# The last output projection in two parts, and the last batch's receptance mixing on VectorE

## The reference

```python
x = x + attn(layernorm(x))        # 16 heads, keys of 16, values of 64, softmax over the queries' axis
x = x + xattn(ctx, ctx, layernorm(x))   # 16 heads of 16, features exp(z) and exp(-z), then fc_w and fc_b
x = x + ffn(layernorm(x))

def ffn(x):                       # x_prev is x shifted by one position, zero first
    xr = mu_r * x + (1.0 - mu_r) * x_prev
    xk = mu_k * x + (1.0 - mu_k) * x_prev
    r = sigmoid(xr @ W_r.T)
    k_act = square(relu(xk @ W_k.T))
    return r * (k_act @ W_v.T)

def attn(x):
    sim = einsum('bnkh,bmhk->bnhm', q, k)
    p = softmax(sim / 4, axis=1)
    o = einsum('bnhm,bmhv->bnhv', p, v)
    return einsum('bnhv,dhv->bnd', o, output_proj)
```

## Time and profile before

| | us |
|---|---|
| median of 3 runs | 449.89 (449.42 to 451.17) |
| the profiled execution's time | 449.9 |
| its span, first to last instruction | 448.1 |
| busy TensorE, VectorE | 426.5, 367.7 |
| busy ScalarE, GpSimd | 300.9, 161.2 |

### The profile page before, as it was taken

One profiled execution on the slowest core, in us unless ns is written; L12 is line 12 of the kernel. 1 busy time (PEld: TensorE's weight loads), 2 busy tenths in 40 slices (PEclk: granted clock), 3 DMA queues, 4 the chain that ended last, 5 costly groups with the idle time before them and its releaser, 6 DMA issues.

```text
span 448.1 us, 8243 instructions
## 1 busy us (share of the span) xinstructions
PE 426.5 (95%) x2738; PEld 274.4 (61%) x2738; DVE 367.7 (82%) x668; ACT 300.9 (67%) x760; POOL 161.2 (36%) x206
## 2 busy tenths in 40 slices
PE   6999999999989999999999999999999999879896
PEld 4745454466545865566655785576555674467775
DVE  4688877798998887888999978798999888669762
ACT  3687988676796666666778566666787757529521
POOL 2163203117232513427052622427331533534442
PEclk9999999999999999999999999999999999999999
DMA  7668302435210015145103002642003100000001
GB/s 241 234 236 269 142 1 96 143 107 197 75 47 1 1 55 179 64 150 187 45 6 119 0 2 103 197 153 91 0 1 111 57 1 1 23 2 1 1 25 47
DMA packets 22561, 38.23 MB, mean 85 GB/s; under 512 B 2808, under 2 KB 7160, under 8 KB 22392
## 3 DMA queue, kind: packets, MB, share of 16 engines
q1 hardware_dynamic: 22520, 37.71, 24.6%
HBM read 23.02 MB, written 14.68 MB: 84 GB/s over the span
## 4 chain that ended last, share of the span: by engine, by line
PE 75%; DVE 9%; ACT 8%; issue 4%; DMA 1%; POOL 1%; SPq 0%; POOLq 0%; ACTq 0%; DVEq 0%
PE av_bank L909 22%; PE m_bank L841 9%; PE s_pair L895 8%; PE m_bank L845 6%; DVE nmax L1355 4%; ACT e_sb L1148 3%; PE m_bank L1045 3%; PE m_bank L961 2%; PE m_bank L1057 2%; PE m_bank L982 2%; PE m_bank L1117 2%; PE m_bank L1106 2%; PE m_bank L926 2%; PE m_bank L1073 2%; PE m_bank L945 1%
## 5 line engine op out<-in xcount | busy, mean ns | idle before, releaser
L1148 ACT ACTIVATE e_sb<-s_pair,nmax 128x512 f32<-128x512 f32 x256 | 174.1, 692 | 62.0 <-DVE nmax L1355 61.8
L1355 DVE TENSOR_REDUCE nmax<-s_pair 128x2 f32<-128x1024 f32 x128 | 152.4, 1213 | 21.5 <-PE s_pair L895 20.6
L909 PE MATMUL av_bank<-e_sb,v_sb 128*64 128x512 f32 x512 | 120.1, 602 | 1.0 <-POOL v_sb L1627 0.8
L1627 POOL TENSOR_TENSOR v_sb<-v_sb,rsum 128x256 f32<-128x256 f32 x64 | 39.7, 622 | 156.6 <-DVE rsum L1363 156.6
L909 PEld LDWEIGHTS av_bank<-e_sb,v_sb 128*64 128x64 f32 x512 | 32.6, 136 | 62.8 <-issue 53.2
L895 PE MATMUL s_pair<-q_st,k_st 64*128 64x512 f32 x256 | 49.9, 456 | 4.8 <-ACT e_sb L1148 4.8
L1148 ACT ACTIVATION_READ_ACCUMULATOR e_sb<-s_pair,nmax 128x1 f32 x256 | 53.6, 209 | 0.0
L895 PEld LDWEIGHTS s_pair<-q_st,k_st 64*128 64x128 f32 x256 | 21.3, 184 | 39.1 <-ACT e_sb L1148 25.2
L841 PE MATMUL m_bank<-wo_hi,ot_hi 128*128 128x256 f32 x128 | 36.4, 290 | 0.0
L845 PE MATMUL m_bank<-wo_lo,ot_hi 128*128 128x256 f32 x128 | 35.0, 279 | 0.0
L1654 POOL TENSOR_TENSOR sx<-sx,xrec 128x512 f32<-128x512 f32 x24 | 24.8, 1045 | 26.9 <-DVE xrec L1541 26.9
(11 more groups left out here) (186 smaller groups left out, 830.9 us busy)
## 6 DMA issues: line engine op xcount, KB each, us to landing
q_st<-q_parts SPq DMA_DIRECT2D x31, 256.0 KB, 3.8
k_st<-k_parts SPq DMA_DIRECT2D x31, 256.0 KB, 3.8
k_parts<-qkt_hi SPq DMA_DIRECT2D x7, 512.0 KB, 3.1
k_parts<-qkt_lo SPq DMA_DIRECT2D x7, 512.0 KB, 4.1
q_parts<-qkt_hi SPq DMA_DIRECT2D x8, 256.0 KB, 2.0
q_parts<-qkt_lo SPq DMA_DIRECT2D x8, 256.0 KB, 2.3
out<-x_sb SPq DMA_DIRECT2D x8, 256.0 KB, 2.2
x_sb<-in_x SPq DMA_DIRECT2D x3, 512.0 KB, 5.0
```

The costliest lines, as they stand in the source:

```text
L909: mm = pe.matmul(av_bank[n % AV_BANKS][64 * par:64 * par + 64, :], v_sb[:, m, 2 * p + par, :], e_sb[:, (4 * q + 2 * i + par) % E_RING, :], ...
L1148: act.activation(e_sb[:, g % E_RING, :], s_pair[k // 2][:, k % 2, :], ACT.Exp, bias=nmax[:, g % 8:g % 8 + 1], accum_out=esum[:, q % 4, k:k ...
L1355: dve.tensor_reduce(nmax[:, at:at + 2], s_pair[i][:, :, :], AX_X, ALU.max, negate=True)\
L1627: pool.tensor_tensor(v_sb[:, m:m + 2, 2 * p:2 * p + 2, :], v_sb[:, m:m + 2, 2 * p:2 * p + 2, :], rsum[:, q % 4, :].rearrange("p (m h) -> p ...
```

## The change

The last output projection (batch 3, second half of the heads) is split into a unit with the first three head pairs and a unit `op_last` with the fourth. For the last batch the receptance mixing leaves GpSimd: VectorE does it in a unit `mix_rec` of its own, with the same two fused instructions as the key mix, and signals `mixr_last`, for which `fr` waits. GpSimd's list has no `mix` for batch 3. All places in `UNITS` and `ATTENTION` are given anew; between the last weighing and the end the lists are as follows (what differs is in brackets, before / after):

- TensorE: op(1,0), [- / op_last(1,0)], op(1,1), [- / filler, op_last(1,1)], t2(0), [one filler / two fillers], z(0), ...; pv(0), [pt(2,0), fc(0), fv of batch 2, pt(2,1), filler / fc(0), pt(2,0), pt(2,1), fv of batch 2], pt(3,0), pt(3,1), t3(0), pv(1), [filler / -], fc(1), fk(0), fr(0), filler, t3(1), fv(0), [four / two] fillers, fk(1), [filler / -], fr(1), fv(1), [two / four] fillers.
- VectorE: ..., mix(0), pv low parts, [- / mix_rec(0)], fc(1), ln3(1), mix(1), [- / mix_rec(1)], fv(0), square(1), fv(1).

Beside attention some units change their places by one to six. For instance, in batch 0 t2(1) goes ahead of weigh 18 and 19 on TensorE, the first statistics of batch 1 ahead of the first reciprocal on VectorE, and batch 1's load ahead of another DMA on SP; near the end, batch 2's mix(1) goes behind the last reciprocal on VectorE.

```diff
-    ("mix", 3, (0,), dict(dve=423, pool=134)),
-    ("mix", 3, (1,), dict(dve=429, pool=137)),
+    ("mix", 3, (0,), dict(dve=423)),
+    ("mix", 3, (1,), dict(dve=430)),
+    ("mix_rec", 3, (0,), dict(dve=426)),
+    ("mix_rec", 3, (1,), dict(dve=431)),
...
     ("op", 3, (1, 0), dict(pe=293, dve=393)),
-    ("op", 3, (1, 1), dict(pe=294, dve=396)),
...
+    ("op", 3, (1, 1), dict(pe=295, dve=396)),
+    ("op_last", 3, (1, 0), dict(pe=294)),
+    ("op_last", 3, (1, 1), dict(pe=297)),
...
-                if before or unit[1] == B - 1:
+                if before or unit[1]:
                     eng.wait_ge(exp_ready, TILES)
...
                 pe.wait_ge(ot_ready, b * NP + 4 * hh + 3)
-                for p in range(4):
-                    if p == 3:
-                        pe.wait_ge(ot_hi_ready, b * NP + 4 * hh + 4)
+                for p in range(3):
                     for t2 in range(2):
...
-                        if p < 3:
-                            pe.matmul(dst, ot_lo[:, p, at:at + P], wo_hi[:, 4 * hh + p, :], start=False, stop=False)
+                        pe.matmul(dst, ot_lo[:, p, at:at + P], wo_hi[:, 4 * hh + p, :], start=False, stop=False)
+                if (b, hh) != (B - 1, 1):
+                    op_last(b, hh, tt)
+
+            def op_last(b, hh, tt):
+
+                unit = ("op", b, (hh, tt))
+                pe.wait_ge(ot_hi_ready, b * NP + 4 * hh + 4)
+                for t2 in range(2):
+                    at = (2 * tt + t2) * P
+                    by_high(bank(unit)[:, t2 * D:(t2 + 1) * D], ot_hi[:, 3, at:at + P], None, wo_hi[:, 4 * hh + 3, :],
+                            wo_lo[:, 4 * hh + 3, :], False, False)
                 pe.wait_ge(ot_ready, b * NP + 4 * hh + 4)
...
-                pe.wait_ge(mixr_ready, 2 * b + half + 1)
+                if b == B - 1:
+                    pe.wait_ge(mixr_last, half + 1)
+                else:
+                    pe.wait_ge(mixr_ready, 2 * b + half + 1)
...
+            def mix_rec(b, half):
+
+                dve.wait_ge(mixk_ready, 2 * b + half + 1)
+                prev = xt3[:, :, half * HALF:(half + 1) * HALF]
+                for c in range(DC):
+                    ins = dve.scalar_tensor_tensor(out=mix_r[:, c, :], in0=mix_r[:, c, :], scalar=mu_sb[:, 0, c:c + 1],
+                                                   in1=prev[:, c, :], op0=ALU.mult, op1=ALU.add)
+                ins.then_inc(mixr_last, 1)
```

More of the change, by code:

```diff
@@ L70 @@
     ("load", 0, ("feat",), dict(sp=0)),
     ("load", 0, ("o",), dict(sp=1)),
[L72 to L78, removed]
+    ("load", 0, ("rest",), dict(sp=13)),
+    ("load", 0, ("x1",), dict(sp=4)),
+    ("mix", 0, (0,), dict(dve=173, pool=48)),
@@ L185 @@
[L185 to L195, removed]
@@ L485 @@
[L485 to L486 removed]
+    dict(scores=14, weigh=21, max=(13, 15), exp=(12, 13, 14, 15), rsum=20, scale=3),
+    dict(scores=17, weigh=22, max=(17, 18), exp=(17, 18, 19, 20), rsum=22, scale=4, ot_hi=28, ot_lo=31),
+    dict(scores=20, weigh=28, max=(23, 24), exp=(22, 23, 24, 25), rsum=30, scale=7),
+    dict(scores=23, weigh=29, max=(26, 28), exp=(29, 30, 31, 32), rsum=32, scale=8, ot_hi=37, ot_lo=39),
@@ new lines @@
+    dict(scores=65, weigh=75, max=(87, 88), exp=(98, 99, 100, 101), rsum=97, scale=23),
+    dict(scores=68, weigh=80, max=(91, 93), exp=(103, 104, 105, 106), rsum=98, scale=25, ot_hi=120, ot_lo=110),
+    dict(scores=72, weigh=84, max=(99, 100), exp=(109, 110, 111, 113), rsum=107, scale=27),
+    dict(scores=76, weigh=85, max=(104, 105), exp=(116, 117, 118, 119), rsum=112, scale=28, ot_hi=128, ot_lo=119),
+    dict(scores=82, weigh=92, max=(111, 113), exp=(122, 123, 124, 125), rsum=120, scale=30),
@@ new lines @@
+    dict(scores=111, weigh=127, max=(152, 154), exp=(169, 170, 173, 174), rsum=167, scale=46),
+    dict(scores=117, weigh=128, max=(160, 161), exp=(179, 181, 183, 184), rsum=170, scale=47, ot_hi=194, ot_lo=177),
+    dict(scores=123, weigh=134, max=(168, 169), exp=(186, 187, 188, 190), rsum=176, scale=49),
+    dict(scores=129, weigh=135, max=(174, 175), exp=(191, 192, 193, 195), rsum=178, scale=51, ot_hi=202, ot_lo=186),
+    dict(scores=133, weigh=141, max=(179, 180), exp=(198, 199, 200, 201), rsum=182, scale=53),
@@ new lines @@
+    dict(scores=158, weigh=170, max=(214, 215), exp=(235, 236, 237, 238), rsum=219, scale=64),
+    dict(scores=162, weigh=173, max=(220, 222), exp=(245, 246, 249, 250), rsum=228, scale=67, ot_hi=260, ot_lo=235),
+    dict(scores=169, weigh=181, max=(227, 229), exp=(254, 255, 256, 258), rsum=232, scale=68),
+    dict(scores=174, weigh=182, max=(233, 234), exp=(263, 264, 265, 266), rsum=239, scale=71, ot_hi=275, ot_lo=249),
+    dict(scores=179, weigh=189, max=(238, 240), exp=(270, 271, 272, 273), rsum=250, scale=73),
@@ L487 @@
+    dict(scores=282, weigh=288, max=(378, 379), exp=(416, 417, 418, 419), rsum=381, scale=118, ot_hi=426, ot_lo=388),
+    dict(scores=286, weigh=291, max=(383, 384), exp=(422, 423, 425, 427), rsum=387, scale=119),
+    dict(scores=289, weigh=292, max=(385, 386), exp=(428, 429, 430, 431), rsum=389, scale=120, ot_hi=432, ot_lo=392),
 ]
```

615 lines of the change are left out of this document (304 added, 311 removed).

## The result

The changed kernel takes 445.12 us (median of 4 runs, 444.12 to 446.11) against 449.65 us of the kernel before (4 runs, 449.18 to 451.17); the ratio is 0.9895, with a 95% interval of 0.9869 to 0.9920. That is 4.5 us less, where 2.6 were forecast: the time lies 1.3 us under the range of the likeliest outcome (446.4 to 448.1), 0.2 us under that of 8 in 10 (445.3 to 449.3), and inside that of rival (c). The profiled execution took 446.03 us (span 444.2), that of before 449.9 (span 448.1).

A forecast was written before the change was run, and what follows sets the result against it. TensorE's queue was taken as the bound from 130 to 365 us, and a chain of latencies over all engines after 390. 449.9 - 1.7 (end) - 0.9 (118 to 130 us) = 447.3 us; likeliest 446.4 to 448.1, 8 in 10 445.3 to 449.3.

The forecast's parts named there:

- the likeliest outcome: Whole kernel: the forecast of 447.3 us itself, with its own range of 446.4 to 448.1 us; chance 0.50.
- rival (c): More is won: the shuffle also takes the stalls at 48 and 65 and part of the 1.4 us: 445 to 446.4; chance 0.11.
- The end (-1.7): Last half of the last batch: receptance mixing on VectorE and fewer fillers let fv start 1.72 us earlier; 1.7 us taken.
- 118 to 130 us (-0.9): Orders laid anew at 118 to 130 us: z(1)'s wait goes, second half of scores 22 starts earlier; 0.9 us gained.
- rival (a): Only the end gains, as VectorE and ScalarE pace the last quads from 365 to 390 us: 448.2 us; chance 0.24.
- The first 50 us (0): Start of the kernel: norm statistics ahead of the first reciprocal delay, other moves help; sum zero, bounds -0.5 (gain) and +2.0.
- The split, the mixing of half 0, the rest of the tail (0): Output projection in two parts, half 0's mix on VectorE, and 397 to 434 us: each counted zero, the tail with ±0.4.
- Everything else (0, ±1): Remaining moves, mainly 130 to 365 us: TensorE can win at most its 1.4 us, the moved reciprocal 0.1; zero, ±1.
- the sign of such a miss: End of attention: prediction wrong if the last projection starts not 0.9 us before 390.16 but later or much earlier.
- rival (b): The beginning loses: the norm ahead of the first reciprocal is not absorbed, +0.7 to 2.0 us, 448.0 to 449.9; chance 0.11.
- Rival (d): Slower: thinned fillers near the end let the clock fall to 1.2 GHz for four units, +6.9 us, 454.2; chance 0.04.

The follow-up runs named there:

- the later one: Second profiled execution of the unaltered changed kernel, run again beside the version with two more fillers: 445.14 us, ratio 0.9898 to the kernel before.

## Why the prediction was wrong

**The end (-1.7): right.** -1.64 in the trace, -1.45 alone, +1.63 when undone. Its steps hold too: fk starts 1.03 us behind the key mix (1.04 worked out), fr has no wait, the square ends 0.2 us ahead of fv, and nothing else becomes late. Half 0 lost nothing.

**118 to 130 us (-0.9): right.** TensorE's idle time there falls by 0.99 us, and the stretch alone wins 0.75 to 0.80 us, which stay until the end; rival (a) is out.

**The first 50 us (0): wrong, by 0.4 to 0.8 us, where the bound on this side was 0.5.** In the 38.58 us from the first matmul to 50 us of before, TensorE's idle time falls from 2.07 to 1.68 us, and the beginning wins 0.4 to 0.8 us. I had put the late norm ahead of the first reciprocal on the path; it is not: with the new orders the first head pairs are 0.60 us ahead, not 0.3 to 0.6 behind.

**The split, the mixing of half 0, the rest of the tail (0): right.** From the end of attention to the last key mix it takes 45.46 to 45.78 us in executions of the changed kernel with or without fillers whose clock did not fall, 45.66 before. I forecast nothing for the split, and using it costs time. The changed kernel without the split wasn't run, so its zero rests on this stretch alone.

**Everything else (0, ±1): the step that failed.** The new orders between 130 and 390 us win 2.1 us by themselves, 1.40 until head pair 27 and 0.74 behind it. The prediction had named the sign of such a miss: attention ends 3.5 us earlier than before (386.74 against 390.28), where 0.9 was forecast. Two sentences of the prediction led to the miss. "Between 130 and 365 TensorE can win no more than its 1.4 us" took the idle time for the whole prize, and then none of that was counted. Until head pair 27 the win is 1.40 us, no more than this bound; but the idle time gave 0.47 us of it, and the busy time, which the sentence takes as work that no order can shorten, 0.93. And "VectorE is the next bound there, so at most 0.1 us" was right for the reciprocal, which alone wins 0.00 us, and for all moves of 360 to 390 us by themselves, which pay for the stall with another of 0.95 us, but it does not hold with the orders ahead of them: from head pair 27 to the last, both the kernel of 130 to 390 us and the changed one win 0.74 us more. That they arrive there with VectorE further ahead is the likely reason (the new wait of 0.95 us is one for VectorE, and it is missing in both); no run takes it apart further. The three gains, 0.4, 0.8 and 2.1 us, make 3.3; together they give 3.05 in the first execution and 2.71 in the later one. As these two differ by 0.34 us themselves, an overlap of the gains isn't shown.

**The sum.** For the median: -3.05 (2.71) in attention and -1.64 at the end make -4.7 (-4.4), and 4.5 was measured. Both kernels have executions with a fallen clock (4 of 10 of the changed one, 31 of 72 of before in the four sets beside the experiments), so the medians pay for it about alike. Single parts timed at full clock give the same: -0.4, -0.6, -1.9 and -1.45 make -4.4, and the changed kernel in its last set has -4.1. Rival (c), more is won at the shuffle, is what happened, though not at 48 us, the reason that I gave first; the wait at 65 us (0.48 us before) is gone. In rival (b) the sum was off: 0.7 to 2.0 us more than 447.3 is 448.0 to 449.3, not 449.9; nothing hangs on it. Rival (d) is wrong in place and size: fillers thinned at the end let no clock fall there (1.00 from 426 us on in the profiled execution), but 1.2 GHz does occur elsewhere, for 3.4 us and at a price of 1.2 to 1.9 us, and in the kernel before as well.

## What to carry to other kernels

TensorE's idle time by the profile is not all that a new order can win: a queue that is 98.7% busy gave 0.93 us out of its busy column beside 0.47 us of idle time. So compare the start of like instructions between two marks, not busy shares, and let both windows start at the same work: a window that starts 0.4 us later in the work shows 0.4 us of gain that isn't there. A bound is no forecast either: I had one of 1.4 us and counted zero of it. A stall that an edit takes away can come back at another wait, as it did in the kernel with the last 25 us alone; such edits have to be tried together with the work in front of them. A list spliced at the wrong place costs more than each of them wins (3.1 us in the trace of the first 50 us alone). A small chain on a slow engine near the end is worth moving together with thinning the fillers that had hidden it: thinning alone won nothing, both won 1.64 us.

## What the runs showed of the hardware

The granted clock fell to its 1.2 GHz level in some executions of the same kernel and not in others, with the same instructions: 4 of 10 executions of the changed kernel have a mean clock of 0.996 and take 1.5 to 1.9 us more, and in one set of runs 11 of 25 of the kernel before did (450.43 against 449.18 us). It fell at 398 us in the changed kernel. In the kernel with only the last 25 us reordered it fell at 127 us, where the orders are those of before; the timeline of TensorE there, and two windows:

```profile
124.50 0.38 PE L1500 MATMUL m_bank<-xt_hi,fm_hi 64*128 64x256 f32 x2 [0.86 <-DVE xt_lo L1950]
126.95 0.50 PE L1367 MATMUL s_pair<-q_st,k_st 64*128 64x512 f32 x2 [1.23 <-ACT e_sb L1620]
...
127.00:128.00 1.00, 1.00 (x6) 0.73 (x6) 0.51 (x1) 1.00 (x4) 0.00 (x0) 0.77 0.00 0
128.00:129.00 1.00, 1.00 (x4) 0.30 (x4) 1.00 (x2) 1.00 (x5) 0.00 (x0) 0.50 0.00 0
```

It falls right behind the two waits of 0.86 and 1.23 us; the kernel before had the same two waits in its profiled execution and kept 1.00. So idle time stands ahead of each of these falls, and does not always bring one. The Trainium skill (TensorE: Matmul & The Clock Gate, Part 1) says that the clock falls when the engine has idled. The traces agree with the direction, but filling one microsecond of idle time ahead of 398 us left the share of such executions at 2 of 6, as without; what decides it in one execution is left open. In the kernel with the first 50 us alone a wait of 2.09 us, from 64.75 to 66.84, was followed by a granted clock of 0.65 in 66 to 70 us.

Beside GpSimd's addition VectorE's square took 1.15 us, alone 0.69: the contention of the earlier trace rows holds for another instruction too.
